# Patch at the origin computed inside the lead of the depthwise stage, its 49 taps as 21 products and 3 sums on VectorE

## What is computed

```python
gate_A = sigmoid(ifft_real(gA_f[None] * x_f))          # 7x7 circular depthwise filter of x
gate_B = sigmoid(ifft_real(gB_f[None] * x_f))          # another one
a_spatial = ifft_real(broadcast_to(A_f[None], (B, H, W, C)))   # the kernel A itself: zero but for 7x7 spots round (0, 0)
b_spatial = ifft_real(B_f[None] * x_f)                 # a third filter
a_t = a_spatial * gate_A
b_t = b_spatial * gate_B
# 8 steps of h = sigmoid(-a_t) * h + sigmoid(a_t) * (softplus(b_t) + 1e-6), as a scan in log space
h_final = jnp.exp(log_h[-1])
return h_final @ W_out + b_out                         # then x = x + this
```

## Time and profile before

| | us |
|---|---|
| median of 3 runs | 5202.73 |
| the three runs | 5195.15, 5208.38, 5202.73 |
| the profiled execution | 5212.34 |
| its span, first to last instruction | 5210.5 |
| depthwise stage, from its first load to the last issue of a store | 4246.24 to 5134.42 |
| origin patch, from its first instruction to the end of the span | 5136.89 to 5210.5 |
| mean granted TensorE clock, share of full speed | 0.951 |

### The profile page before, as it was taken

The page is one execution under the profiler, slowest core; times in us unless marked ns, Lnnn a source line. Parts: engine busy times, 40 slices in busy tenths (PEclk is TensorE's granted clock), DMA queues, the critical chain, the costliest instruction groups (busy, mean ns, idle before and its releaser), DMA issues. The chain is left out here.

```text
span 5210.5 us, 111216 instructions
## 1 busy us (share of the span) xinstructions
PE 4694.4 (90%) x38054; PEld 3497.3 (67%) x38054; DVE 3439.8 (66%) x10158; ACT 2855.5 (55%) x6303; POOL 1979.7 (38%) x1397
## 2 busy tenths in 40 slices
PE   6999999999999998758999899997399979999972
PEld 5777777777777776536777667774144459888972
DVE  7887888788887887614666656663288844555564
ACT  0888888888888887013333333333144424555551
POOL 1666666666666664012233223331044411222221
PEclk8999999999999999968999999998699989999985
DMA  7222222222222222984222222226667779999972
GB/s 291 68 72 71 71 70 71 70 70 70 71 72 72 71 71 63 377 290 133 67 70 67 81 68 68 68 66 256 223 196 235 235 269 328 336 330 331 335 232 55
DMA packets 826733, 789.53 MB, mean 152 GB/s; under 512 B 62816, under 2 KB 703033, under 8 KB 817625
## 3 DMA queue, kind: packets, MB, share of 16 engines
q1 hardware_dynamic: 804266, 740.90, 45.5%
q10 hardware_dynamic: 18304, 28.26, 1.5%
q0 software_dynamic: 3616, 13.35, 0.7%
HBM read 574.59 MB, written 207.68 MB: 150 GB/s over the span
## 5 line engine op out<-in xcount | busy, mean ns | idle before, releaser
L299 POOL TENSOR_TENSOR at_bias<-at_tri,at_mask 128x1024 f32<-128x1024 f32 x512 | 1204.6, 2377 | 749.6 <-DVE at_neg_max L460 738.7
L409 ACT ACTIVATE at_probs<-at_neg_s,at_neg_max 128x256 f32<-128x256 f32 x2048 | 894.7, 502 | 0.1
L460 DVE CUSTOM_DVE_ANT_0 at_neg_s<-at_p_s,at_bias 128x256 f32<-128x256 f32 x2048 | 744.2, 420 | 47.1 <-PE at_p_s L333 47.1
L344 PE MATMUL at_p_t<-all_ident,at_probs 128*128 128x128 f32 x4096 | 628.2, 276 | 0.3 <-ACT at_probs_t L401 0.2
L344 PEld LDWEIGHTS at_p_t<-all_ident,at_probs 128*128 128x128 f32 x4096 | 483.9, 141 | 136.6 <-issue 84.6
L1714 PE MATMUL dw_p_conv<-dw_xw,dw_wts 128*128 128x128 f32 x4096 | 510.3, 277 | 70.4 <-issue 49.8
L927 ACT ACTIVATE ml_h<-ml_p,l_b 128x512 f32<-128x512 f32 x384 | 263.9, 687 | 556.1 <-PE ml_p L886 556.1
L1714 PEld LDWEIGHTS dw_p_conv<-dw_xw,dw_wts 128*128 128x128 f32 x4096 | 480.7, 190 | 89.1 <-issue 87.1
L468 DVE COPY at_probs_t<-at_p_t 128x512 f32<-128x512 f32 x512 | 352.6, 689 | 203.2 <-PE at_p_t L344 203.2
L895 PE MATMUL ml_p<-l_w1s,ml_h 128*128 128x128 f32 x4096 | 478.4, 275 | 0.8 <-issue 0.8
L895 PEld LDWEIGHTS ml_p<-l_w1s,ml_h 128*128 128x128 f32 x4096 | 467.8, 192 | 3.1 <-issue 3.1
(11 more groups left out here) (229 smaller groups left out, 8977.3 us busy)
## 6 DMA issues: line engine op xcount, KB each, us to landing
dw_wts<-patch_w SPq DMA_DIRECT2D x256, 512.0 KB, 8.1
dw_xw<-planes SPq DMA_DIRECT2D x128, 528.0 KB, 6.2
sp_xs<-x SPq DMA_DIRECT2D x128, 512.0 KB, 9.0
planes<-pw_plane SPq DMA_DIRECT2D x128, 264.0 KB, 2.9
in_xs<-in_x_dram SPq DMA_DIRECT2D x32, 1024.0 KB, 7.7
at_xs<-in_x_dram SPq DMA_DIRECT2D x256, 128.0 KB, 2.3
at_kvs<-in_L_conv_kv_x_dram SPq DMA_DIRECT2D x256, 128.0 KB, 2.6
at_mask<-in_L_conv_mask_bias_dram SPq DMA_DIRECT2D x256, 128.0 KB, 3.3
```

Source lines behind the costliest of these rows:

```text
L299: pool.tensor_tensor(bias[:, n % 2, part], tri[:, part], mask[:, n % 4].unsqueeze(1).broadcast_to((128, 4, COLS)), ALU.add).then_inc(maske ...
L344: mm = pe.transpose(p_t[h % 2][:, kh, qh * 128:(qh + 1) * 128], probs[:, h, qh, kh * 128:(kh + 1) * 128], ident[:, :])
L409: e = act.activation(probs[:, h, qh, :], neg_s[:, n % 2, h, qh, :], ACT.Exp, bias=neg_max[:, n % 2, i:i + 1], scale=-1.0)
L460: t = dve.tensor_tensor_reduce(neg_s[:, n % 2, h, qh, :], p_s[h][:, qh, :], bias[:, n % 2, i, :], -1.0, 3.0e38, ALU.add, ALU.min, neg_max[ ...
```

## The change

The block of `origin_patch` is gone, and its steps stand between those of the lead of `depthwise_layer`:

- **Loads.** ScalarE issues the 53 + 2 small loads of the pixels and the two kernels, as the first thing that it does in the stage, after a wait for GpSimd's clearing of the tile. GpSimd issues the other 16. SyncE's queue of windows and weights is untouched.
- **Taps.** VectorE writes the taps in reverse order to `og_flip` (14 copies), then for each filter 7 products of 128 x 343 elements (7 taps of a row at once, for all 49 pixels, into the idle second half of `raw`), and then 3 sums over 49 x 49 elements. 21 products and 3 sums stand for 147 multiply-adds.
- **Places.** Window and flips after the copy of group 6; products after 8, 10 and 12; sums after 14; further steps after 16, 20, 26 and 32. ScalarE's steps follow its copies of groups 17 and 23. TensorE transposes the pixels after conv(5) and projects after conv(30).
- **Stores.** 8 of the 14 stores go out in unit 40 of SyncE's queue, the other 6 behind the wait for the stage's last stores.
- The small tiles lie in the first half of `hid`, the PSUM tiles are `p_turn[0]` and `p_out[0]`; all are idle in the lead.

```diff
-def depthwise_layer(nc, x3t, planes, patch_w, ksum, scale, shift, w_plain, b_plain, ident, out):
+def depthwise_layer(nc, x3t, planes, patch_w, ksum, scale, shift, w_plain, b_plain, ident, out,
+                    a_kernel, gate_a_kernel, taps, w_out, b_out):
...
+        products = raw[:, 1, CH // 2:, :].rearrange("p c s -> p (c s)")
...
+            def store_origin(lines):
+                for i in lines:
+                    y = (i - HALO) % ROWS
+                    sp.dma_start(out[0, y, COLS - HALO:COLS], og_final[i * SIDE:i * SIDE + HALO, :]).then_inc(og_stored, 16)
+                    sp.dma_start(out[0, y, 0:HALO + 1], og_final[i * SIDE + HALO:(i + 1) * SIDE, :]).then_inc(og_stored, 16)
...
+                if u == 40:
+                    sp.wait_ge(og_final_ready, 1)
+                    sp.wait_ge(stored[0], 64)
+                    sp.wait_ge(stored[2], 64)
+                    store_origin(range(HALO, SIDE))
             for s in range(4):
                 sp.wait_ge(stored[s], 64 * (total // 4))
+            store_origin(range(HALO))
+            sp.wait_ge(og_stored, 32 * SIDE)
...
+            def turn_origin():
+                pe.wait_ge(og_cells, 16 * (len(pieces) + 2))
+                for i in range(2):
+                    mm = pe.transpose(p_turn[0][:, i, :], og_xs[:, i, :], ident[:, :])
+                mm.then_inc(og_turned, 1)
...
         def _(act):
+            act.wait_ge(og_cleared, 1)
+            for at, y, x, k in pieces:
+                act.dma_start(og_xs[at % 128:at % 128 + k, at // 128, :], tokens_at(y, x, k)).then_inc(og_cells, 16)
+            for i, kn in enumerate((a_kernel, gate_a_kernel)):
+                act.dma_start(og_kern[:, i, :], kn.rearrange("c a b -> c (a b)")).then_inc(og_cells, 16)
             act.preload_act_table_set(EXP_LN_SET)
...
+            def origin_products(f):
+                dve.wait_ge(og_step, og_done)
+                field = og_win.rearrange("p a b -> p (a b)")
+                grid = products[:, f * KTAPS * KTAPS:(f + 1) * KTAPS * KTAPS].rearrange("p (a b t) -> p a b t", b=SIDE, t=KTAPS)
+                for ty in range(SIDE):
+                    row = field[:, (SIDE - 1 - ty) * span:(SIDE - 1 - ty) * span + 1]
+                    patches = bass.AP(row.tensor, row.offset, [row.ap[0], [span, SIDE], [1, SIDE], [1, SIDE]])
+                    tap = og_flip[:, f, ty * SIDE:(ty + 1) * SIDE].unsqueeze(1).unsqueeze(1).broadcast_to((128, SIDE, SIDE, SIDE))
+                    mul = dve.tensor_tensor(grid[:, :, :, ty * SIDE:(ty + 1) * SIDE], patches, tap, ALU.mult)
+                chained(mul)
+
+            def origin_sums():
+                dve.wait_ge(og_step, og_done)
+                for f in range(3):
+                    grid = products[:, f * KTAPS * KTAPS:(f + 1) * KTAPS * KTAPS].rearrange("p (a t) -> p a t", t=KTAPS)
+                    chained(dve.tensor_reduce(og_conv[:, f, :], grid, mybir.AxisListType.X, ALU.add))
+                chained(dve.tensor_scalar(og_add[:, 0:2], ksum[:, :], shift, None, ALU.mult))
+                chained(dve.tensor_scalar(og_add[:, 2:3], og_sum, shift, None, ALU.mult))
...
-def origin_patch(nc, x3t, a_kernel, gate_a_kernel, taps, ksum, scale, shift, w_out, b_out, ident, out):
...
-            for tap in range(KTAPS):
-                ty, tx = divmod(tap, SIDE)
-                dve.wait_ge(dve_step, done)
-                for f, k in enumerate((taps[:, 0, tap:tap + 1], taps[:, 1, tap:tap + 1], kern[:, 1, tap:tap + 1])):
-                    chained(dve.scalar_tensor_tensor(
-                        out=grid(conv[:, f, :]), in0=field[:, SIDE - 1 - ty:2 * SIDE - 1 - ty, SIDE - 1 - tx:2 * SIDE - 1 - tx],
-                        scalar=k, in1=grid(conv[:, f, :]), op0=ALU.mult, op1=ALU.add))
```

More of the change, by code:

```diff
@@ L1602, with origin_pieces @@
 PLAIN = 1.0 - 0.5 ** SCAN
-def depthwise_layer(nc, x3t, planes, patch_w, ksum, scale, shift, w_plain, b_plain, ident, out):
+def origin_pieces():
+    span = SIDE + 2 * HALO
+    pieces = []
+    for row in range(span):
+        y = (row - 2 * HALO) % ROWS
+        for x, first, left in ((COLS - 2 * HALO, 0, 2 * HALO), (0, 2 * HALO, SIDE)):
+            at = row * span + first
+            while left:
+                k = min(left, 128 - at % 128, PATCH - (x + SHIFT) % PATCH)
+                pieces.append((at, y, x + SHIFT, k))
+                at, x, left = at + k, x + k, left - k
+    return span, pieces
+def depthwise_layer(nc, x3t, planes, patch_w, ksum, scale, shift, w_plain, b_plain, ident, out,
+                    a_kernel, gate_a_kernel, taps, w_out, b_out):
     groups = CH // 4
@@ new lines, in origin_gated, with origin_gate @@
+            def origin_gated():
+                dve.wait_ge(og_step, og_done)
+                for f in range(2):
+                    chained(dve.tensor_scalar(og_gated[:, f, :], og_conv[:, f, :], scale, og_add[:, f:f + 1], ALU.mult, ALU.add))
+                dve.tensor_scalar(og_gated[:, 2, :], og_conv[:, 2, :], scale, og_add[:, 2:3], ALU.mult, ALU.add
+                                  ).then_inc(og_conv_ready, 1)
+            def origin_gate():
+                dve.wait_ge(og_sig_ready, 1)
+                chained(dve.tensor_tensor(og_bt, og_gated[:, 0, :], b_sig, ALU.mult))
+                chained(dve.tensor_tensor(og_gate, og_kern[:, 0, :], a_sig, ALU.mult))
+                dve.wait_ge(og_step, og_done)
+                dve.scalar_tensor_tensor(out=og_soft, in0=og_bt, scalar=-1.0, in1=og_bt,
+                                         op0=ALU.mult, op1=ALU.max).then_inc(og_gate_ready, 1)
@@ L1858, in _, with origin_final @@
+            def origin_final():
+                dve.wait_ge(og_out_made, 1)
+                dve.wait_ge(og_rest, 16 * (2 + 2 * SIDE))
+                chained(dve.tensor_tensor(og_final[:, :], p_out[0][0:KTAPS, 0, :], og_bias, ALU.add))
+                dve.wait_ge(og_step, og_done)
+                dve.tensor_tensor(og_final[:, :], og_final[:, :], og_res, ALU.add).then_inc(og_final_ready, 1)
             for g in range(0, lead, 2):
                 copy_raw(dve, g, dve.tensor_copy, even_copied)
+                if g == 6:
+                    origin_window()
+                if 8 <= g < 14:
+                    origin_products(g // 2 - 4)
+                if g == 14:
+                    origin_sums()
+                if g == 16:
+                    origin_gated()
+                if g == 20:
+                    origin_gate()
+                if g == 26:
+                    origin_hidden()
+                if g == 32:
+                    origin_final()
@@ L2094, in build @@
             coefficients("l3", stats)
[L2095 to L2096 removed]
+        depthwise_layer(nc, x3t, planes, patch_w, ksum, scale, shift, w_plain[:, :], b_plain[:, :], ident, out,
+                        a_kernel, gate_a, taps, w_out, b_out)
 def constants():
```

235 lines of the change are left out of this document (96 added, 139 removed).

## The result

The median of the change is 5154.26 us, that of before, measured beside it, 5202.96 us. One of the four executions behind the first median was a slow one at a lower clock (5227.1), and all ratios and intervals here leave such executions out; the other three gave 5144.8, 5149.6 and 5158.9. The ratio is 0.9901, interval 0.9878 to 0.9925: some 51 us less. The forecast was 58.0 us less and 5144.7; the time lies in the stated range of 5130 to 5164, 9.6 us above the forecast. The profiled execution has a span of 5157.1 us, 53.4 less than before.

What follows compares the result with a forecast made beforehand. The origin patch was taken as a serial tail of 73.6 us. Terms -70.2 + 7.1 + 3.1 + 1.0 + 1.0 = -58.0 us gave 5144.7 us on the median 5202.73 (chance 0.75), range 5130 to 5164.

Steps and rivals of the forecast that it cites:

- The tail: End of the kernel: the serial origin patch leaves, only six stores and the close remain, and the end comes 70.2 us earlier.
- ScalarE's issues: Start of the depthwise stage: 55 issues at 0.32 us delay table load and first copy; TensorE stands still 7.1 us.
- B: Rival at the stage's start: full queues slow ScalarE's 55 issues to 1.03 us apiece, 39.1 us more, 5183.8; chance 0.06.
- A: Rival at the stage's start: ScalarE's issues cost nothing, being over early or their loss won back; 5134.5 us; chance 0.12.
- The clock: TensorE after its first stop: conv(2) and conv(3) run at the low 1.2 GHz level, costing 3.1 us.
- The small loads: Behind conv(5): TensorE's wait for the patch's pixels is covered, the last being issued at 4264.2; no cost.
- Rival C: Behind conv(5): small loads land one after another at 1.8 us, TensorE waits for the last; 5213.5 us, slower; chance 0.04.
- VectorE's products, flips and window: In VectorE's pauses between copies in the lead: seven products take 3.1 us, window and flips likely fit; no cost.
- The three sums: Behind group 14's copy: sums of 2.64 us each overrun the pause by 3.9 us, mostly won back; 1.0 us taken.
- The stores in unit 40: SyncE's queue in unit 40: eight extra stores cost between 0 and 2.5 us; 1.0 taken.

Runs made afterwards that it cites:

- issues moved: The change with ScalarE's table load and logarithm first, 28 small loads next, the rest behind its first four copies, patch steps later; 5144.83 us, 0.9891; sent again 5147.11 us, 0.9888.
- sums one at a time: The change with its three sums drawn apart, one each behind the copies of groups 14, 16 and 18, and later steps moved on; ratio 0.9899.
- early stores by GpSimd: The change with ScalarE's small loads moved behind its table load and copies, sums drawn apart, and GpSimd issuing the 8 early stores; 5144.72 us, ratio 0.9878.
- the filler: The change plus 36 unread products of the identity with itself on TensorE behind conv(1), in the first stop; one run, 5155.56 us.

## Why the prediction was right, and where it was off

The prediction was right in its direction and its mechanism, and the time is in the range. The gain was 4.6 us smaller in the profile than the sum (53.4 against 58.0), and about 7 by the ratio. The terms that were added to the tail came to 12.2 us; measured they come to 17.9 to 18.6, against 17.0 that all ahead of the tail gained, and what lies between them is within the scatter of the middle. Term by term:

- **The tail, -70.2.** Measured -70.4: 5.7 us stand behind the last result's issue, where 5.9 (1.8, 1.9, 2.2) were forecast. In the kernel without the patch 2.8 us stand there, so six stores cost 2.9.
- **ScalarE's issues, +7.1.** Measured 9.2. The chain was right, the price was not: 55 issues took 19.4 us, 0.35 each instead of SyncE's 0.32. That is 1.8 us; the remaining 0.3 lie in pauses between the steps of the chain. I took the lower bound because the transfers were the same, and the engine and the load around them were not. B (1.03 us) and A are both ruled out, the latter by moving the issues. So the Trainium skill's remark in "DMA: Bandwidth & Descriptors" (Issuing engines are not separate DMA queues), that the time to start a transfer is usually small beside the transfer, does not carry over to 2 KB loads ahead of a table load.
- **The clock, +3.1.** Measured 1.9: only conv(2) ran at the low level. The direction, which the Trainium skill gives in "TensorE: Matmul & The Clock Gate" (What's actually happening), agrees with the granted clock of 0.51; the sum took the pair conv(0), conv(1) as the pattern, of which conv(1) at 0.65 was no pattern.
- **The small loads.** No wait, as forecast: the transposes ran at 4277.40 directly behind conv(5). Rival C is out. But loads by GpSimd took 5.0 to 5.3 us to land beside the stage's transfers, and the last kernel load, of 24.5 KB, 5.5 to 6.3 until the transposes that waited for it, not the 1.2 us of the quiet tail; they overlap, so the stage only notices when their last is issued 6 us before it is needed. With the issues moved, the transposes behind conv(9) waited 2.2 to 2.5 us in all four executions, and those behind conv(11) did not.
- **VectorE's products, flips and window.** Fit, as forecast: 3.06 us for seven (3.1). The sums took 2.64 us each, forecast to the hundredth.
- **The three sums, +1.0. This is the step that failed; they cost 5.6 in this profile, and 4.9, 4.0 and 3.6 in the three others with the same sums.** The sentence was: "loads go on for these 3.9 us, and TensorE then finds full tiles and wins back 0.42 us in each of 8 pairs." TensorE stood still for 3.63 us. Against before, the even copies were 10.8 us late ahead of the stop and 14.9 behind it; two pairs of groups won back 1.0 us, then the tiles were empty and 2.6 us were lost: 16.4. The reason is a sentence of the prediction itself, used for ScalarE's stop and forgotten here: SyncE may not issue weights g before conv(g-4) is done. Its queue shows no issue between 4303.74 and 4309.97, and what was on its way lasted only to about 4309. Then the transfers missed: 113 GB/s from 4308 to 4312 and 267 from 4312 to 4318, where 384 were usual, is 2.8 + 1.8 = 4.6 us of transfer time, near the 5.6 that were lost (that the one makes up the other is argued, not tried). A second term was left out altogether: the clock fell in this stop as well, and conv(18) took 3.45 us instead of 1.79, 1.7 more. This prolongs the time in which SyncE may not issue. One sum at a time took both away: no run dry of the transfers, no fall of the clock.
- **The stores in unit 40, +1.0.** 1.2 to 1.9 by the means of the traces; right within what the scatter of the middle lets one see.

The 10.8 us ahead of the sums are the first two terms (9.2 + 1.9 is 11.1). What stays open is why the same three sums cost 3.6 us in one execution and 5.6 in another. Open too is what makes the middle scatter by 14 us from one execution to the other, since it does so without the patch too.

## What to carry to other kernels

Work that is put beside a pipeline has to fit between two of its steps: the same three sums cost 3.6 to 5.6 us in one piece and under 1 us as three pieces, and the same 55 issues cost 11 us ahead of a table load and little behind the copies. When a stop is costed, ask first what refills the buffers during it; if the loads wait for the engine that has stopped, nothing refills them and the stop isn't won back behind it. And read the stage, not the total, where the rest scatters by more than the edit is worth.

## What the hardware showed that I had not expected

The granted clock is decided by more than whether TensorE is busy at the moment. A stop of 3.63 us at full clock was followed by 3 us at 0.50. Stops of 1.86 us (sums one at a time), 2.34 us (early stores by GpSimd) and 2.52 us (issues moved) left it at 1.00. But one of 2.63 us, behind the filler, left it at 1.00 for the first part of conv(2), and it fell to 0.50 with TensorE busy; and one of 3.59 us at the sums (issues moved, sent again) was followed by 1 us at 1.00 and then by 3 us at 0.50. So a clock that is still full when the engine resumes does not show that the stop was free. And a small load that is cheap to issue is late to land beside heavy transfers: a kernel load of 24.5 KB, issued at 4270.78, was waited for until 4277.07, and GpSimd's loads of 1.5 and 2 KB took 5.0 to 5.3 us, while the last of the 71 in the quiet tail, one of 2 KB, had landed 1.2 us after its issue.
